# Middle attention's GpSimd operations in two halves of eight heads; threshold candidates formed ahead and counted in bf16

## What is computed

```python
q = _layernorm(q, qn_w, qn_b)
k = _layernorm(k, kn_w, kn_b)
attn = jax.nn.softmax(jnp.einsum('bhqd,bhkd->bhqk', q, k) * scale, axis=-1)
out = jnp.einsum('bhqk,bhkd->bhqd', attn, v)
```

```python
scores = jax.nn.softmax(xt @ wg, axis=-1)
top_scores, sel = jax.lax.top_k(scores.T, CAPACITY)   # CAPACITY = 1024
```

## Time and profile before

| | us |
|---|---|
| median of 3 runs | 1705.91 |
| lowest, highest of them | 1703.36, 1707.97 |
| the profiled execution: time | 1705.25 |
| the profiled execution: span, first to last instruction | 1703.5 |

### The profile page before, as it was taken

How to read it: one execution, slowest core, us unless ns; L and a number is a source line. 1 busy time by engine, 2 the same in 40 slices (tenths; PEclk the granted TensorE clock), 3 DMA queues, 4 the chain that set the end, 5 groups by cost and what they waited for, 6 DMA issues and landing times. The chain is left out here.

```text
span 1703.5 us, 25226 instructions
## 1 busy us (share of the span) xinstructions
PE 1450.4 (85%) x9452; PEld 1209.0 (71%) x9452; DVE 1088.8 (64%) x2302; ACT 750.5 (44%) x1293; POOL 638.8 (38%) x437
## 2 busy tenths in 40 slices
PE   6997669998859999996899987669999999499774
PEld 4886558887459999995677765347888888368632
DVE  6776667975456676773464553576766665467487
ACT  2553535443137676762444342113334343145465
POOL 2461225566024455541132222022665564244100
PEclk9998979999979999997899998889999999799897
DMA  5000000000356777755000000413544443500001
GB/s 187 1 2 5 1 1 1 1 1 1 114 182 198 219 225 223 224 139 126 16 1 1 1 1 1 138 54 111 103 98 97 88 93 44 117 1 2 1 1 50
DMA packets 94175, 122.01 MB, mean 72 GB/s; under 512 B 12300, under 2 KB 79271, under 8 KB 94055
## 3 DMA queue, kind: packets, MB, share of 16 engines
q1 hardware_dynamic: 72935, 91.56, 16.7%
q0 software_dynamic: 21120, 28.85, 9.4%
HBM read 94.95 MB, written 25.43 MB: 71 GB/s over the span
## 5 line engine op out<-in xcount | busy, mean ns | idle before, releaser
L2563 POOL DMA_INDIRECT ch_total<-ch_y,ch_index x64 | 107.1, 1674 | 123.3 <-DVE ch_y L2750 108.3
L1208 POOL DMA_INDIRECT t_total<-t_y,t_index x46 | 98.1, 2132 | 133.9 <-DVE t_y L1327 108.6
L3565 POOL TENSOR_TENSOR L_s<-L_s,L_mx 128x1232 f32<-128x1232 f32 x32 | 76.5, 2389 | 125.8 <-DVE L_mx L3649 125.8
L2687 ACT ACTIVATE ch_silu<-ch_ps 128x512 f32<-128x512 f32 x64 | 38.3, 598 | 169.6 <-PE ch_ps L738 169.6
L736 PE MATMUL ch_ps<-ch_hT_hi,ch_w_hi 128*128 128x512 f32 x256 | 103.7, 405 | 10.4 <-DVE ch_hid L2776 7.0
L736 PE MATMUL t_ps<-t_hT_hi,t_w_hi 128*128 128x256 f32 x368 | 106.9, 290 | 6.0 <-DVE t_w_lo L1315 6.0
L736 PE MATMUL t_ps<-t_w_hi,t_act_hi 128*128 128x256 f32 x368 | 105.8, 288 | 0.0
L737 PE MATMUL t_ps<-t_hT_lo,t_w_hi 128*128 128x256 f32 x368 | 105.7, 287 | 0.0
L738 PE MATMUL t_ps<-t_hT_hi,t_w_lo 128*128 128x256 f32 x368 | 105.6, 287 | 0.0
L737 PE MATMUL t_ps<-t_w_lo,t_act_hi 128*128 128x256 f32 x368 | 104.1, 283 | 0.0
L738 PE MATMUL t_ps<-t_w_hi,t_act_lo 128*128 128x256 f32 x368 | 104.1, 283 | 0.0
(11 more groups left out here) (562 smaller groups left out, 4406.7 us busy)
## 6 DMA issues: line engine op xcount, KB each, us to landing
t_w_in<-in_L_ffn_w1T SPq DMA_DIRECT2D x23, 1024.0 KB, 5.3
t_w_in<-in_L_ffn_w2T SPq DMA_DIRECT2D x23, 1024.0 KB, 5.7
ch_w_in<-in_L_ffn_w SPq DMA_DIRECT2D x24, 512.0 KB, 4.0
x<-in_x SPq DMA_DIRECT2D x4, 512.0 KB, 4.9
t_total<-x SPq DMA_DIRECT2D x1, 2048.0 KB
t_rows<-t2d_h SPq DMA_DIRECT2D x1, 2048.0 KB
x<-t_total SPq DMA_DIRECT2D x8, 256.0 KB, 4.5
tb_w<-in_L_xattn_w SPq DMA_DIRECT2D x2, 1024.0 KB, 9.7
```

What stands on the lines that cost most here:

```text
L1208: nc.gpsimd.indirect_dma_start(out=total, out_offset=bass.IndirectOffsetOnAxis(ap=index[:, 2 * j + u:2 * j + u + 1], axis=0), in_=y[:, j % ...
L2563: nc.gpsimd.indirect_dma_start(out=total, out_offset=at(s, u), in_=y[:, s % 2, u, :], in_offset=None, compute_op=ALU.add).then_inc(added[s ...
L3565: nc.gpsimd.tensor_tensor(s[:, n % G], s[:, n % G], spread(mx[:, n % G, :], 2, [P, H, KEYS]), ALU.subtract).then_inc(shifted, 1)
```

## The change

In wide_attention each of GpSimd's three operations is issued as two instructions of eight heads (616 columns) each, one behind the other; the semaphore is still incremented once, after the second.

In choose_tokens own and counts become bf16 (a count is at most 128, own is 0 or 1), and counts and cand get two buffers. While TensorE adds the counts, VectorE forms `follow`, the 4 x 4 candidates of the next step for each outcome of this one, and shifts pair. Then L2416's counterpart multiplies follow (4 x 4) by the test, and the reduction gives the next step's four candidates themselves, so that the OR between the reduction and the counts is gone. The last step does as before. Four more memsets stand ahead of the loop.

```diff
+            HALVES = (slice(0, H // 2), slice(H // 2, H))
+
             def add_bias(n):
                 pool.wait_ge(s_taken, 2 * n + 2)
-                flat = s[:, n % 3].rearrange("p h n -> p (h n)")
-                nc.gpsimd.tensor_tensor(flat, flat, kb[:, n // BT, :], ALU.add).then_inc(biased, 1)
+                for hs in HALVES:
+                    own = s[:, n % 3, hs, :].rearrange("p h n -> p (h n)")
+                    ins = nc.gpsimd.tensor_tensor(own, own, kb[:, n // BT, hs.start * KEYS:hs.stop * KEYS], ALU.add)
+                ins.then_inc(biased, 1)
+
+            def by_row(n, row, op):
+                for hs in HALVES:
+                    ins = nc.gpsimd.tensor_tensor(s[:, n % 3, hs, :], s[:, n % 3, hs, :],
+                                                  spread(row[:, n % 3, hs], 2, [P, H // 2, KEYS]), op)
+                return ins
...
                 pool.wait_ge(max_ready, n + 1)
-                nc.gpsimd.tensor_tensor(s[:, n % 3], s[:, n % 3], spread(mx[:, n % 3, :], 2, [P, H, KEYS]), ALU.subtract
-                                        ).then_inc(shifted, 1)
+                by_row(n, mx, ALU.subtract).then_inc(shifted, 1)
...
                 pool.wait_ge(recip_ready, n + 1)
-                nc.gpsimd.tensor_tensor(s[:, n % 3], s[:, n % 3], spread(den[:, n % 3, :], 2, [P, H, KEYS]), ALU.mult
-                                        ).then_inc(probs_ready, 1)
+                by_row(n, den, ALU.mult).then_inc(probs_ready, 1)
...
-                nc.tensor.matmul(ps_c[:, 0:VALUES + 1], own[:], counts[:], start=True, stop=True).then_inc(total_ready, 1)
+                nc.tensor.matmul(ps_c[:, 0:WAYS], own[:], counts[:, step % 2, :], start=True, stop=True
+                                 ).then_inc(total_ready, 1)
...
             for step in range(BIT_PAIRS):
-                chain.wait()
-                chain(nc.vector.tensor_tensor(cand[:].bitcast(I32), thr[:].bitcast(I32).broadcast_to([P, VALUES + 1]),
-                                              pair[:], ALU.bitwise_or))
+                own_cand, next_cand = cand[:, step % 2, :], cand[:, (step + 1) % 2, :]
+                last_step = step == BIT_PAIRS - 1
                 chain.wait()
                 for v in range(VALUES):
-                    nc.vector.tensor_scalar(hit[:, v, :], lane_probs[:], cand[:, v + 1:v + 2], None, ALU.is_ge, ALU.add,
-                                            accum_out=counts[:, v + 1:v + 2]).then_inc(count_ready, 1)
-                chain(nc.vector.tensor_scalar(pair[:], pair[:], 2, None, ALU.logical_shift_right))
+                    nc.vector.tensor_scalar(hit[:, v, :], lane_probs[:], own_cand[:, v + 1:v + 2], None, ALU.is_ge, ALU.add,
+                                            accum_out=counts[:, step % 2, v + 1:v + 2]).then_inc(count_ready, 1)
+                if not last_step:
+                    chain(nc.vector.tensor_tensor(follow[:].bitcast(I32), spread(own_cand.bitcast(I32), 1, ways),
+                                                  spread(pair[:], 2, ways), ALU.bitwise_or))
+                    chain.wait()
+                    chain(nc.vector.tensor_scalar(pair[:], pair[:], 2, None, ALU.logical_shift_right))
                 dve.wait_ge(total_ready, step + 1)
...
+                else:
+                    chain(nc.vector.scalar_tensor_tensor(out=passed[:], in0=spread(ps_c[:, 0:WAYS], 1, ways),
+                                                         scalar=float(CAPACITY), in1=follow[:], op0=ALU.is_ge, op1=ALU.mult))
+                    chain.wait()
+                    chain(nc.vector.tensor_reduce(next_cand, passed[:], AX.X, ALU.max))
```

More of the change, by code:

```diff
@@ L2248, in choose_tokens @@
     lane_probs, hit = sb("lane_probs", [P, P]), sb("hit", [P, VALUES, P])
-    apart, own = sb("apart", [P, P], I32), sb("own", [P, P])
-    pair, cand, thr = sb("pair", [P, VALUES + 1], I32), sb("cand", [P, VALUES + 1]), sb("thr", [P, 1])
-    counts, passed, thr_wide = sb("counts", [P, VALUES + 1]), sb("passed", [P, VALUES + 1]), sb("thr_wide", [P, P])
+    apart, own = sb("apart", [P, P], I32), sb("own", [P, P], BF16)
+    WAYS = VALUES + 1
+    pair, cand = sb("pair", [P, WAYS], I32), sb("cand", [P, 2, WAYS])
+    follow, passed = sb("follow", [P, WAYS, WAYS]), sb("passed", [P, WAYS, WAYS])
+    counts, thr, thr_wide = sb("counts", [P, 2, WAYS], BF16), sb("thr", [P, 1]), sb("thr_wide", [P, P])
     count, need = sb("count", [P, E]), sb("need", [P, E])
@@ L2385, in _ @@
             low = 1 << (2 * BIT_PAIRS - 2)
[L2386 to L2389, removed]
+            for v in range(WAYS):
+                chain(nc.vector.memset(cand[:, 0, v:v + 1].bitcast(I32), v * low))
+                chain(nc.vector.memset(pair[:, v:v + 1], v * (low >> 2)))
+            for n in range(2):
+                chain(nc.vector.memset(counts[:, n, 0:1], float(P)))
             dve.wait_ge(logits_psum, NG)
@@ L2404, in _ @@
             chain(nc.vector.tensor_copy(lane_probs[:], ps_p))
+            ways = [P, WAYS, WAYS]
             for step in range(BIT_PAIRS):
-                chain.wait()
-                chain(nc.vector.tensor_tensor(cand[:].bitcast(I32), thr[:].bitcast(I32).broadcast_to([P, VALUES + 1]),
-                                              pair[:], ALU.bitwise_or))
+                own_cand, next_cand = cand[:, step % 2, :], cand[:, (step + 1) % 2, :]
+                last_step = step == BIT_PAIRS - 1
@@ L2410, in _ @@
                 chain.wait()
                 for v in range(VALUES):
-                    nc.vector.tensor_scalar(hit[:, v, :], lane_probs[:], cand[:, v + 1:v + 2], None, ALU.is_ge, ALU.add,
-                                            accum_out=counts[:, v + 1:v + 2]).then_inc(count_ready, 1)
-                chain(nc.vector.tensor_scalar(pair[:], pair[:], 2, None, ALU.logical_shift_right))
-                dve.wait_ge(total_ready, step + 1)
-                chain(nc.vector.scalar_tensor_tensor(out=passed[:], in0=ps_c[:, 0:VALUES + 1], scalar=float(CAPACITY),
-                                                     in1=cand[:], op0=ALU.is_ge, op1=ALU.mult))
@@ L2418, in _ @@
-                chain.wait()
-                chain(nc.vector.tensor_reduce(thr[:], passed[:], AX.X, ALU.max))
+                    nc.vector.tensor_scalar(hit[:, v, :], lane_probs[:], own_cand[:, v + 1:v + 2], None, ALU.is_ge, ALU.add,
[5 more added lines that the diff above has]
+                    chain(nc.vector.tensor_scalar(pair[:], pair[:], 2, None, ALU.logical_shift_right))
@@ new lines, in _ @@
+                dve.wait_ge(total_ready, step + 1)
+                if last_step:
+                    chain(nc.vector.scalar_tensor_tensor(out=passed[:, 0, :], in0=ps_c[:, 0:WAYS], scalar=float(CAPACITY),
+                                                         in1=own_cand, op0=ALU.is_ge, op1=ALU.mult))
+                    chain.wait()
+                    chain(nc.vector.tensor_reduce(thr[:], passed[:, 0, :], AX.X, ALU.max))
+                else:
+                    chain(nc.vector.scalar_tensor_tensor(out=passed[:], in0=spread(ps_c[:, 0:WAYS], 1, ways),
+                                                         scalar=float(CAPACITY), in1=follow[:], op0=ALU.is_ge, op1=ALU.mult))
+                    chain.wait()
+                    chain(nc.vector.tensor_reduce(next_cand, passed[:], AX.X, ALU.max))
```

## The result

| | us |
|---|---|
| changed kernel, median of 20 runs | 1700.11 (1693.58 to 1706.43) |
| kernel before, on the same chip, median of 20 runs | 1704.52 (1698.95 to 1709.11) |
| ratio, 95% interval | 0.9972 (0.9962 to 0.9982) |
| profiled execution after: time, span | 1704.78, 1703.0 |

The ratio is worth -4.8 us (-6.5 to -3.1) where -5.9 was forecast. A single execution scatters by more than the whole effect, and the two profiled spans differ by only 0.5 us, so this pair of traces has to be read stage by stage.

The account below looks back on a forecast made before the run. TensorE, busy 85% of the span, was taken to bound the kernel, the threshold search being an uncovered chain. Attention -1.7 and search -4.2 gave -5.9 us from the median 1705.91: 1700.0, range 1696.0 to 1705.0.

Parts of the forecast that it names:

- Split: GpSimd operations in attention: each split into halves costs 0.145 us, 0.44 us a tile; bounds 0 and 0.727.
- Even turns: Attention turns 2, 4, 6: normalise gets in 1.3 us earlier, TensorE's 0.87 us wait for divide goes; -2.6 us in all.
- Rival 1: Attention: VectorE does not get in between the halves, only the splits' cost stays; -3.3 us, 1702.7; chance 0.12.
- L588 between the halves: Attention, even turns: this small VectorE operation may slip in between divide's halves, lengthening divide by 0.18 us.
- Turn 11: Attention turn 11, without normalise: L749 waits for shift's later second half, so attend(12) is later; +0.4 us.
- Turns 13 and 14: Late attention: split add_bias, divide and shift follow one another, delaying tile 15's exponential and attend(14); +0.44 us.
- Attention in all: Sum of the attention's terms: -2.6 + 0.4 + 0.44 + 0.1 = -1.7 us; bounds -2.6 and +1.0.
- Search, the OR: Threshold search: one chained 0.19 us operation gone, less 0.013 on each of two left; net -0.165 us a step.
- The product's pass: Threshold search: a single bf16 pass replaces two float32 passes, saving 0.13 us a step; bounds 0 and 0.26.
- Rival 3: Search: the saved pass is worth its whole record, 0.26 us; -7.6 us in all, 1698.3; chance 0.17.
- Rival 2: Search gives the OR's saving only, bf16 pass no quicker or follow sticking out; -4.0 us, 1701.9; chance 0.17.
- rival 4: Attention: a GpSimd instruction's fixed part is large, to 0.727 us a split; +0.6 us, 1706.5; chance 0.04.

Follow-up runs that it names:

- e3: Kernel before with the changed choose_tokens and only add_bias in halves, divide and shift whole: ratio 0.9954 (0.9935 to 0.9972), -7.8 us.
- e4: Kernel before with the changed choose_tokens, GpSimd's operations whole, normalise(n+8) moved behind denominators(n+1) on VectorE: ratio 0.9954 (0.9937 to 0.9970), -7.8 us.
- e5: Kernel before with the changed choose_tokens, but own and counts left in float32; executed once: search 27.62 us, 1.78 us a step.
- e6: Kernel before with only own and counts in bf16, candidates formed as before; executed once: search 26.99 us, 1.75 us a step.
- e7: Kernel before with GpSimd's three attention operations in four parts of four heads, search as before; one execution: attention stage 206.39 us.
- e8: e3 with add(n-1) ahead of take(n+2) on VectorE from turn 12 on: ratio 0.9980 (0.9963 to 0.9997) against the kernel before.

## Why the prediction was right, and where not

The median came out at 1700.11 where 1700.0 was forecast, and the two stages gave -6.0 us where -5.9 was summed. That the medians agree to 0.1 us is luck: the forecast started from 1705.91, the kernel before had 1704.52 beside the changed one, and the measured change is -4.8. The sum of the stages is right because two errors in it cancel, which is luck too: the attention gave 1.1 less than its -1.7, the search 1.2 more than its -4.2.

*Split.* 0.145 us each was forecast. The halves lasted 1.509 and 1.217 us where 1.49 and 1.22 were said; two of add_bias take 0.20 more than one whole where normalise gets in between (3.03 to 2.83) and 0.14 to 0.16 where nothing does, two of divide 0.14 (2.39 to 2.25). The widths of the earlier trace rows were the right rows. The page on GpSimd that the prediction set against them (the Trainium skill, GPSIMD Engine Reference, Instruction dispatch) led to 0.04; no trace here agrees with that as the price of a split, and quarters confirm 0.19 fixed.

*Even turns.* -0.87 each was forecast, limited by TensorE's own wait. From take(0) turn_probs(3), (5) and (7) come earlier by 1.01, 1.96 and 2.88 us (60.17 to 59.16 for the first). 0.06 of that is there before turn 2, so it is 0.94 each and 2.8 in all, 0.2 more than the waits of the earlier trace rows held. The reading that TensorE is late from 316.98 on, the end of attend(4)'s record, came 0.16 too late. In e3 turn_probs(5) starts at 314.61, 4.33 us behind attend(4)'s start, while attend(4)'s record lasts 4.49: the records of products overlap, and a wait shows as idle time only beyond the overlap. In the changed kernel the distance is 4.42, and the weight load waits for divide (0.33), so divide, with its split and L596 in it, still ends last there. With divide whole, e3 and e4 gain 1.09 a turn. Rival 1, that VectorE isn't let in, is refuted by normalise's 1.51 us.

*L588 between the halves* (L596 now) was forecast at 0.18 and cost 2.62 - 2.39 = 0.23. By the other page (the Trainium skill, SBUF — State Buffer, A bandwidth-pool intuition that's wrong) it would have been 0.475, an estimate. The trace agrees with that page that the loser waits out the other's whole instruction (normalise, 2.81 and 1.51 us), and not with such a price for one guest between two GpSimd instructions.

*Turn 11* was to cost 0.4 and cost 0.2: from take(0) take(14) is 2.66 us earlier, where turn_probs(7) was 2.88. L755 took 1.14 instead of 2.17, since it now gets in after shift's first half, and L757 waited out the second with 1.15. *Turns 13 and 14* were to cost 0.44; the exponential of tile 15 is 2.25 earlier, so 0.4. *The opening*, +0.1 forecast, was -0.06, less than it moves between two executions of the kernel before (0.27).

*The term that failed in the attention* is "Attention in all": it has no clock in it. The parts named add up to -2.88, the opening included, + 0.22 + 0.42 = -2.24 us; attend(14)'s 1.68 us bring that to the stage's -0.56. The earlier trace rows showed a warning that I read only as a wait: attend(12), behind 2.81 us of idle TensorE, took 6.24 us for the 20 products that took 4.49 in the earlier trace rows, at a granted clock of 0.73.

*Search, the OR*: -0.165 a step forecast, 0.17 by e5. *The product's pass* is the term that was mis-sized. I took the 0.13 by which the second pass started behind the first. The step fell by 0.20, as e6 shows by itself: a lone bf16 product takes 0.18 us against 0.39 for the pair. From the product's start to the test it is 0.42 us before and 0.22 in e6 and after. No pass of the kernel before stands alone: the 0.170 in the earlier trace rows is the first of a pair in one of the first steps, and the median of 0.263 lies between first passes of 0.273 and second ones of 0.253. So the earlier trace rows could not give the price of a lone one. Rival 3 held as to its direction, with 1.58 us a step between the forecast's 1.66 and its own 1.53. *follow* costs nothing, as said, since the 0.22 is the same with it (after) and without it (e6); its margin, forecast at 0.06 us, was used to the last hundredth. The first steps are the smaller part of the difference: twelve periods of 0.374 are 4.5 us, and the first ones with the ends gave 0.9, where 0.7 stood (0.4, 0.19, 0.13).

Rival 2, the OR alone, and rival 4, slower by a large fixed part, have fallen: the step is not 1.78 us and the fixed part is not 0.7.

## What to carry to other kernels

When one instruction of another engine shuts a small one out, split the instruction that does so, or move the small one behind the chain, and leave its neighbours whole: each split costs about its fixed part, here 0.14 to 0.20 us, and pays only where someone stands waiting. In a sum for TensorE's path give a price to the clock behind every stretch where TensorE idles and whose timing moves, as an open term in the range, since here it took 1.7 of the 2.2 us won. Idle time in the rows of overlapping products understates how much earlier they could start, here by 0.16 us a turn. For a tiny chained product compare whole chains (last input to result) and not the records of passes that overlap.

## What the runs showed of the hardware that was not expected

TensorE's granted clock under the same 20 products was 1.00 or 0.73 depending on a schedule that differed by a few tenths of a microsecond, and that was the same in each repeat of a kernel. The products then take 4.59 or 6.27 us, in e7 and e8 7.50 and 7.43 (clock 0.60 and 0.61). attend(12) took 6.21 to 6.25 us wherever it waited 2.7 to 2.8 us for add, and 4.56 us in e7 and e8, where it waited 2.34 and 1.40. For attend(14) the traces give no such simple rule.
